# Value products of four heads issued together, and the second attention's first batches prepared inside the first

## The reference, cut to what matters

```python
h = layernorm(x) * (1 + ca) + sa
x = x + ga * attn0(h)      # 8 heads of 16, 4 kv heads; causal, window 128 and 4 sinks
h = layernorm(x) * (1 + cb) + sb
x = x + gb * ffn0(h)       # rmsnorm; attn1: 16 heads of 8, 4 kv heads, causal; rmsnorm; top-2 of 8 experts
h = layernorm(x) * (1 + ca1) + sa1
x = x + ga1 * attn2(h)     # 16 heads of 8, 16 kv heads, no mask
h = layernorm(x) * (1 + cb1) + sb1
x = x + gb1 * ffn1(h)      # top-1 of 8 experts, capacity
# in each attention
attn = softmax(q @ k.T * scale);  y = (attn @ v) @ Wo
```

## Time and profile before

| | us |
|---|---|
| median of three timed runs | 1655.85 |
| lowest, highest | 1653.58, 1659.35 |
| the profiled execution | 1657.83 |
| its span in the trace | 1655.9 |
| PE busy in the span | 1349.0 (81%) |
| DVE busy | 889.0 (54%) |
| ACT busy | 691.7 (42%) |
| mean granted clock of PE | 0.892 |

### The profile page before, as it was taken

The page is one execution under the profiler, slowest core; times in us unless marked ns, Lnnn a source line. Parts: engine busy times, 40 slices in busy tenths (PEclk is TensorE's granted clock), DMA queues, the critical chain, the costliest instruction groups (busy, mean ns, idle before and its releaser), DMA issues.

```text
span 1655.9 us, 30043 instructions
## 1 busy us (share of the span) xinstructions
PE 1349.0 (81%) x9552; PEld 922.4 (56%) x9552; DVE 889.0 (54%) x2395; ACT 691.7 (42%) x1575; POOL 553.2 (33%) x820
## 2 busy tenths in 40 slices
PE   5899999968898898898865895788888877887494
PEld 3677677646666666566644784444444444443272
DVE  2555555435555545645655564566666666566213
ACT  2344444423454454344352452255554544444231
POOL 2222222132222222354351003354454545633242
PEclk9899999959999999899986997598898988788697
DMA  8223222100000000000011432000000000020144
GB/s 285 85 89 112 79 79 83 43 13 4 8 5 7 7 5 8 4 22 17 18 58 53 98 87 70 7 8 23 12 21 15 17 19 20 20 66 14 35 130 129
DMA packets 75997, 77.73 MB, mean 47 GB/s; under 512 B 9488, under 2 KB 57904, under 8 KB 75472
## 3 DMA queue, kind: packets, MB, share of 16 engines
q1 hardware_dynamic: 69712, 63.31, 12.2%
q0 software_dynamic: 6144, 12.63, 2.6%
HBM read 37.50 MB, written 38.40 MB: 46 GB/s over the span
## 4 chain that ended last, share of the span: by engine, by line
PE 60%; DVE 17%; POOL 8%; issue 8%; ACT 3%; DMA 2%; DVEq 0%; SPq 0%; POOLq 0%; ACTq 0%
PE ps_out L2176 11%; PE ps_max L2096 6%; DVE row_max L1891 5%; PE ps_work L2033 4%; PE ps_four L2122 3%; PE ps_four L1243 3%; PE ps_four L2008 3%; PE ps_max L2086 3%; PE ps_four L2086 2%; PE ps_four L2013 2%; PE ps_max L1262 2%; PE ps_four L2033 2%; POOL rstd L1486 2%; PE ps_max L1327 2%; PE ps_four L1318 2%
## 5 line engine op out<-in xcount | busy, mean ns | idle before, releaser
L1891 DVE TENSOR_REDUCE row_max<-ps_max 128x3 f32<-128x384 f32 (+1 forms) x640 | 370.3, 603 | 130.3 <-PE ps_max L2096 125.1
L1726 ACT ACTIVATE attn_f<-ps_four 128x384 f32<-128x384 f32 (+1 forms) x640 | 331.3, 532 | 252.6 <-PE ps_four L2122 251.3
L2096 PE MATMUL ps_max<-k_st,q_st 24*128 24x256 f32 (+2 forms) x1280 | 272.0, 349 | 63.8 <-DVE row_max L1891 56.2
L2176 PE MATMUL ps_out<-attn_f,v_all 128*9 128x256 f32 (+3 forms) x2560 | 316.9, 372 | 1.1 <-ACT attn_f L1716 0.8
L2096 PEld LDWEIGHTS ps_max<-k_st,q_st 128*128 128x128 f32 (+1 forms) x1280 | 182.2, 206 | 125.0 <-DVE row_max L1891 74.6
L2122 PE MATMUL ps_four<-q_st,k_st 26*128 26x256 f32 (+2 forms) x1280 | 242.3, 325 | 0.0
L2176 PEld LDWEIGHTS ps_out<-attn_f,v_all 128*9 128x9 f32 (+1 forms) x2560 | 101.6, 94 | 137.2 <-issue 33.7
L2122 PEld LDWEIGHTS ps_four<-q_st,k_st 128*128 128x128 f32 (+1 forms) x1280 | 172.0, 201 | 3.7 <-ACT attn_f L1726 1.7
L2086 PE MATMUL ps_max<-masks,ident_bf 128*128 128x256 bf16 (+1 forms) x384 | 119.0, 310 | 38.2 <-DVE row_max L1891 33.7
L1512 POOL TENSOR_TENSOR split<-rope_ab 128x256 fp32r<-128x256 f32 (+1 forms) x80 | 57.7, 722 | 262.2 <-DVE rope_ab L1809 262.2
L2086 PE MATMUL ps_four<-masks,ident_bf 128*128 128x256 bf16 (+1 forms) x384 | 118.2, 308 | 2.7 <-ACT attn_f L1726 1.8
(11 more groups left out here) (290 smaller groups left out, 2351.6 us busy)
## 6 DMA issues: line engine op xcount, KB each, us to landing
slots_dram<-attn_f SPq DMA_DIRECT2D x72, 256.0 KB, 3.1
h_words<-slots_dram SPq DMA_DIRECT2D x72, 64.0 KB, 1.8
y_dram<-y_tok SPq DMA_DIRECT2D x36, 128.0 KB, 1.8
wd<-in_L_ffn_W SPq DMA_DIRECT2D x16, 256.0 KB, 2.8
mod<-mod_dram SPq DMA_DIRECT2D x16, 192.0 KB, 3.2
slots_dram<-attn_f SPq DMA_DIRECT2D x8, 260.0 KB, 4.4
h_words<-slots_dram SPq DMA_DIRECT2D x8, 260.0 KB, 3.0
x_all<-in_L_attn_x SPq DMA_DIRECT2D x8, 256.0 KB, 6.9
```

What stands on the lines that cost most here:

```text
L1726: nc.scalar.activation(probs[:, h % 4, 0:w], ps_exp[:, h % 3, 0:w], ACT.Exp, scale=c.scale).then_inc(exp_done, 1)
L1891: nc.vector.tensor_reduce(row_max[:, r2, 0:blocks, h], src, AX_X, ALU.max).then_inc(max_done, 1)
L2096: ins = nc.tensor.matmul(bank[:, at:at + keys.stop], q_st[rows, r, g, k * P:(k + 1) * P], k_st[rows, r, c.k_group(h), keys], start=not c.c ...
L2176: last = nc.tensor.matmul(ps_out[base:base + c.hd + 1, at + first:at + S], v_tok[c.index][:, r, kb, h // (c.heads // c.kv), :], probs[:, h ...
```

## The change

`pair_values` becomes `four_values`: heads 4p to 4p+3 in four column groups, in one row of sixteen records. The fours of a batch stand in slots 5, 9 and 13 (attention 0: only 5), and the last in slot 1 of the next batch. `probs` keeps its four places, and exp(h) its wait.

```diff
-            def pair_values(c, b, r, p):
-                pe.wait_ge(exp_done, HEADS_BEFORE[c.index] + b * c.heads + 2 * p + 2)
-                if p % 4 == 0:
-                    at_least(pe, strips_out, strip_groups_until(c, b - 1) + p // 4)
+            def four_values(c, b, r, p):
+                pe.wait_ge(exp_done, HEADS_BEFORE[c.index] + b * c.heads + 4 * p + 4)
+                if p % 2 == 0:
+                    at_least(pe, strips_out, strip_groups_until(c, b - 1) + p // 2)
...
                 for kb in range(BLK):
                     first = P if c.causal and kb == 1 else 0
-                    for h in (2 * p, 2 * p + 1):
+                    for h in range(4 * p, 4 * p + 4):
...
-                last.then_inc(values_mm, 2)
+                last.then_inc(values_mm, 4)
...
                     if h == 1 and flags(b)[0]:
-                        pair_values(c, b - 1, (r - 1) % RING, c.pairs - 1)
-                    if h % 2 and h > 2:
-                        pair_values(c, b, r, (h - 3) // 2)
+                        four_values(c, b - 1, (r - 1) % RING, c.heads // 4 - 1)
+                    if h % 4 == 1 and h > 1:
+                        four_values(c, b, r, h // 4 - 1)
```

```diff
+        SEAM = ["stat", "xhat", "sq", "turn0", "hn", "ht", "ot", "q", "k", "y", "v", "sel0", "sel1", "sel2", "rows", "sel3",
+                "place0", "place1"]
+        def later(c, b, by):
+            if c.index == 0 and isinstance(b, int) and b + by >= NB:
+                return CFGS[1], b + by - NB
+            return c, b + by
...
+            if c.index == 0:
+                names = names if later(c, b, 2)[0] is c else SEAM
+                with_prep = with_next = True
...
                 elif name in MAXIMA:
-                    maxima(c, b + 1, (r + 1) % RING, name)
+                    maxima(*later(c, b, 1), (r + 1) % RING, name)
                 else:
-                    prep(c, b + 2, (r + 2) % RING, name)
+                    prep(*later(c, b, 2), (r + 2) % RING, name)
...
             def start(c):
+                if c.index == 1:
+                    return
...
+                    if h == 1 and c.index == 0 and is_batch(b, NB - 2):
+                        load_select(CFGS[1])
...
+                if c.index == 0 and is_batch(b, NB - 2):
+                    pe.wait_ge(rotated, 2)
+                    pe.wait_ge(loads_late, 16 * len(late_loads))
+                    pe.wait_ge(ones_ready, 4)
```

More of the change, by code:

```diff
@@ L1577, in segment @@
                     gather_pair(pool, b + 3, (r + 3) % RING)
[L1578 removed]
+                if c.index == 0 and is_batch(b, NB - 2):
+                    pool.wait_ge(x_done, b - 1)
+                    ones_row(CFGS[1])
+                for h, (_, before, behind) in enumerate(slots(c, b)):
                     walk(c, b, r, post, prep, maxima, before + behind)
@@ L1719, in segment @@
                 w = c.q_cols()
-                for h, (_, before, behind) in enumerate(slots(c, *flags(b))):
+                for h, (_, before, behind) in enumerate(slots(c, b)):
                     walk(c, b, r, post, prep, maxima, before)
@@ L1953, in segment @@
             def segment(c, b, r):
-                for h, (max_heads, before, behind) in enumerate(slots(c, *flags(b))):
+                for h, (max_heads, before, behind) in enumerate(slots(c, b)):
                     for i, k in max_heads:
-                        head_max(c, b + 1, (r + 1) % RING, i, k)
+                        head_max(*later(c, b, 1), (r + 1) % RING, i, k)
                     walk(c, b, r, post, prep, maxima, before)
@@ L2288, in finish @@
             def finish(c):
-                pair_values(c, NB - 1, (NB - 1) % RING, c.pairs - 1)
+                four_values(c, NB - 1, (NB - 1) % RING, c.heads // 4 - 1)
                 names = [n for n in post_names(c) if n not in NO_PE]
-                post_step, _, _ = tracked({bank_of(c, n): reader_of(c, NB - 2, n) for n in names})
+                free = {bank_of(c, n): reader_of(c, NB - 2, n) for n in names}
+                if c.index == 0:
+                    free = {bank_of(CFGS[1], name): reader_of(CFGS[1], 0, name) for name in ("place0", "place1")}
+                post_step, _, _ = tracked(free)
                 for name in names:
```

56 lines of the change are left out of this document (34 added, 22 removed).

## The result

The changed kernel takes 1697.07 us, the median of four runs (1691.39 to 1705.07), against 1657.6 for the kernel before in the same sessions (four runs, 1653.58 to 1663.87). The ratio is 1.0238, 95% interval 1.0175 to 1.0301: slower by some 40 us, where 22 were forecast. The profiled execution took 1702.65 us, a span of 1700.7, so it lies 45 us above that of before.

A forecast was written before the change was run, and what follows sets the result against it. PE was taken to set the pace in the first two attentions and share it with DVE in the third. Terms 1 + 8 + 19 - 13 - 15.4 + 22 = +21.6 gave 1679.4 us on the trace, 1678 median; range 1625 to 1750.

The forecast's parts named there:

- A four costs what a pair costs: Value products: four column groups run together, 0.76 or 0.98 us to the next start, leaving PE 136 us less work.
- rival 4: Value products: four column groups run two at a time, a four lasting two pairs; 1745 to 1813 us, chance 0.08.
- Exponentials held by the four: ACT's queue: exp(4), exp(8), exp(12) and the next exp(0) wait for the four, with copies of PE's work banks behind them.
- First attention, +1 forecast: Steady batches of the first attention: stalls and the removed pair's saving net +0.1 us a batch, 14 batches, +1.
- the 0.9 by which the last add of row maxima was to be later: First attention, batch end: DVE's last add, which released the next exp(0)'s scores, comes 0.9 us later.
- The seam, -15.4 forecast: Between first and second attention: preparation carried by batches 14 and 15 takes 54.8 us in place of 70.2.
- Second attention, +8 and +11 for the clock forecast: Second attention: stalls of +0.5 us a batch over 16 batches, +8, and a granted clock 0.03 lower.
- Third attention, +17 forecast (19, -13 and 11): Third attention: late batch ends +19 us, pairs removed at half clock -13, and a granted clock 0.03 lower.
- up to slot 11 it is even: Third attention, batch up to slot 11: each step losing a pair ends in a wait for DVE or POOL, no net change.
- the -13 for pairs at half clock: Third attention: about one removed pair a batch lies where PE sets the pace at half clock, 16 times 0.8 us saved.
- Seam only: Whole kernel: ACT's backlog is absorbed and the clock stays, leaving the seam's -15.4; about 1640 us, chance 0.17.
- The clock falls: Second and third attention: PE's thinner stream lowers the clock by 0.10, 74 us in place of 22; about 1730, chance 0.10.

The follow-up runs named there:

- e1: The changed kernel with its value products in pairs again at their old slots, the seam's change kept: 1640.5 us, ratio 0.9898.
- e5: The changed kernel, four places for probabilities, with every four one slot earlier (slots 4, 8, 12 and 0 of the next batch): 1637.88 us, ratio 0.9873.
- e6: The changed kernel with every four one slot earlier and eight places for probabilities in the third attention: 1634.47 us, ratio 0.9862.
- e3: The changed kernel with eight places for probabilities in the third attention, PE's instructions the same: 1662.63 us, ratio 1.0047.
- e12: e9 with the third attention's pairs streaming 128 of 256 query columns from its second batch on, so not a whole kernel: 1615.72 us against 1622.15.
- e9: The changed kernel with fours one slot earlier in the first and second attention and pairs in the third, four places: 1622.15 us, ratio 0.9813.

## Why the prediction was right, and where it was not

The range, 1625 to 1750, held 1697, and the direction was right. The sum was 23 us short of the profiled run (1679.4 against 1702.65; less the 2 us it is 1677 for the median, not 1678). That it came out as near is luck: the third attention was forecast 40 us too low, and the first and second together 19 too high. Point by point:

**A four costs what a pair costs: right.** 1.04 and 0.83 were forecast, 1.05 and 0.84 measured. The reading of the earlier trace rows, four row strips that start together, carried over to column groups. On rival 4: the Trainium skill (TensorE: Matmul & The Clock Gate, Part 3 on packing small matmuls) gives 2.38 times for three column tiles; here four heads in 1.05 us against a serial product of 1.08 is a factor of 4.1. Its strict order of starts and ends doesn't bring the result that I had drawn from it: four records start together at 1180.03.

**Exponentials held by the four: right, with the place named.** ACT's idle time moved to L2206, 500.0 us, in bursts behind each four.

**First attention, +1 forecast, -5.3 measured.** The step that failed is a size, the 0.9 by which the last add of row maxima was to be later. The rows of the changed kernel, where the four at 138.39 answers to the pair at 121.88 in the earlier trace rows:

```profile
138.39 0.84 PE L2206 MATMUL ps_out<-attn_f,v_all 128*17 128x256 f32 x16
139.37 0.49 ACT L1749 ACTIVATE attn_f<-ps_four 128x384 f32<-128x384 f32 x1 [3.40 <-PE ps_out L2206]
...
140.06 0.74 PE L2063 MATMUL ps_four<-split,select 128*128 128x256 f32 x4 [0.83 <-ACT v_all L1665]
...
140.64 0.65 PE L2063 MATMUL ps_work<-split,select 65*128 65x256 f32 x4
...
144.06 0.68 DVE L1934 TENSOR_TENSOR q_st<-q_st,ps_work 128x512 fp32r<-128x512 f32 x1
```

sel1 waited 0.83 for v's copy, as worked out. But sel2 followed at once at 140.64, where I had it wait for sel0's cast: the cast started at 139.90, before sel1. The add came 5.67 after the product in place of 5.32, which is 0.35 and not 0.9. With the 0.76 of the pair gone from slot 3 that makes 0.41 less a batch: 18.1 us, where 18.6 was forecast.

**The seam, -15.4 forecast, -13.1 measured.** In e1 and e5 it took 54.4 and 54.9 against 54.8 forecast; in the changed kernel 57.6 at a clock of 0.81. One term of the 54.8 was added up short: from 335.01 to 338.23 and y's 1.20 are 4.4 and not 3.8.

**Second attention, +8 and +11 for the clock forecast, +6.3 measured.** The stalls came at the places named: rlog (L2103) waited for ACT 13 times, 9.8 us, and ht's wait for DVE grew from 14.0 to 23.8 us (read from 16 us after the attention's start, the changed kernel first).

```profile
PE ps_work L2030 <- DVE h_both L1822: 23.8, 13, 2.3
PE ps_work L2103 <- ACT k_st L1674: 9.8, 13, 0.8
```

```profile
PE ps_work L2003 <- DVE h_both L1797: 14.0, 12, 1.6
```

The clock fell by 0.04, where I took 0.03. Which term was 13 us too large the trace doesn't tell singly; e5 and e6 differ by 9 us here with equal instructions, so much of the miss is no larger than what moves without any change.

**Third attention, +17 forecast (19, -13 and 11), +56.5 measured.** Two steps failed. The end of the batch, worth 19, went in the forecast's direction: the scores' wait for DVE's last add grew from 2.6 to 13.2 us, 13 times at most 1.2. First, though, "up to slot 11 it is even": I looked for the late ACT only at the copies that empty the work banks, and took the score banks as free. There the scores of two heads go out together, and those behind each four need the bank of a held exponential. That was 32.7 us of new waits, and e3 without them is 37.5 shorter. Second, the clock: I took 0.03 off, as for the second attention, between nothing and the 0.10 that two stretches of the trace before differ by, and near the lower end. It fell by 0.20. The step took the second and third attention to be equally far from the half clock. The third was already there in part, with products of 1.88 beside ones of 1.04, and there e12 shows a fall of 0.10 for 48 us less of products; while the first attention, at 1.00, lost half of its products' stream too (43.2 us to 22.0) and kept its clock. It is also where the -13 for pairs at half clock went: the products did get 50 us shorter, but the others' 64 came with it. (By its own working the term was short too: 0.8 is what the half clock adds to a pair, and one that sets the pace there would give its whole 1.88.)

**The rivals.** "Seam only" (1640) is what pairs (e1, 1640.5) gave. "The clock falls" named the mechanism and gave 0.10 to a fall of 0.10; its 1730 was for both attentions, where the second lost 0.04 and the third 0.20.

What stays open: how the 56.5 us divide between waits and clock. Taking the held exponentials away gives 37.5, but in e5 the clock rose to 0.77 with them gone and as much idle time as before, while in e3 it stayed at 0.69 with 21 us less of it. So the amount of products and of idle time doesn't settle the clock alone. The mean clock can't be turned into time either: in the second attention the others took 325.4 us at 0.92 in the changed kernel and 313.7 at 0.90 in e9. The two causes aren't independent, and no run here holds the clock fixed.

## What to carry to other kernels

Where a wait is given a coarser grain (four heads released together, in place of two), lay the release before the next user's turn and not behind it: the same fours one slot earlier are worth 59 us here. And before PE time is taken out, read the granted clock of the stretch: at 1.00 the clock stayed and half of the saving reached the end (11 of 21 us), at 0.86 half of it went to the other matmuls and an eighth reached the end (6 of 48), so use the shorter form where the clock is full and leave the longer one where it is not.

## What the runs showed of the hardware

Two value products issued one behind the other, each in two column groups of its own, overlap fully: sixteen records last 1.06 us, as one pair's eight last 1.04. The clock answers to PE's stream in both directions: 50 us more of value products brought it from 0.69 to 0.88, and 48 less from 0.86 to 0.76, with slots, places and counts unchanged. But it doesn't answer to the stream alone: the same instructions a slot earlier went from 0.66 to 0.77, with as much idle time of PE (126.5 and 127.1 us).
